# Four-image attention pipeline on one core: output products ordered by PSUM banks, with one bank finished by TensorE and ScalarE

## The reference

```python
x_proj = jnp.einsum('mc,bchw->bmhw', w_in, x)             # 128 channels -> 16
fs = fftshift(fft2(x_proj, norm='ortho'))
mag_avg = abs(fs).mean(axis=1)                            # energy by angle, 90 bins
# two strongest angles of an image choose a region; gain is 1.2, 1.0 or 0.8
fs_enh = fs * gain[:, None, :, :]
x_enh = ifft2(ifftshift(fs_enh), norm='ortho').real
out = jnp.einsum('cm,bmhw->bchw', w_out, x_enh)           # 16 -> 128 channels
return x + out
```

## Time and profile before

| | us |
|---|---|
| median of 3 runs | 278.42 (278.32 to 278.46) |
| the profiled execution | 278.63 |
| its span | 276.8 |
| TensorE busy | 264.9 |
| ScalarE busy | 184.7 |
| VectorE busy | 174.3 |
| the eight transfers to `out`, issue to landing, each | 2.1 |

### The profile page before, as it was taken

How to read it: one execution, slowest core, us unless ns; L and a number is a source line. 1 busy time by engine, 2 the same in 40 slices (tenths; PEclk the granted TensorE clock), 3 DMA queues, 4 the chain that set the end, 5 groups by cost and what they waited for, 6 DMA issues and landing times.

```text
span 276.8 us, 4058 instructions
## 1 busy us (share of the span) xinstructions
PE 264.9 (96%) x1328; PEld 157.1 (57%) x1331; DVE 174.3 (63%) x297; ACT 184.7 (67%) x355; POOL 63.3 (23%) x97
## 2 busy tenths in 40 slices
PE   7999999999999999999999999988999998899993
PEld 2864666457655665563667535844545546664573
DVE  4686769687645743276776978777325247646773
ACT  1584477887887667665787577988846758647430
POOL 2016018300400002537821300110003607500000
PEclk9999999999999999999999999999999999999999
DMA  5990000000000010000000000000000000000026
GB/s 170 281 305 3 0 0 4 23 26 26 4 0 0 0 54 2 0 1 1 3 0 1 0 2 1 4 1 0 0 1 0 2 0 4 1 1 2 1 78 227
DMA packets 4573, 8.52 MB, mean 31 GB/s; under 512 B 1250, under 2 KB 2018, under 8 KB 4554
## 3 DMA queue, kind: packets, MB, share of 16 engines
q1 hardware_dynamic: 4554, 8.27, 9.1%
HBM read 5.60 MB, written 2.10 MB: 28 GB/s over the span
## 4 chain that ended last, share of the span: by engine, by line
PE 87%; ACT 4%; DVE 3%; DMA 2%; issue 1%; SPq 0%; DVEq 0%; ACTq 0%
PE psum L366 84%; DMA qs<-row 2%; DMA xin<-in_x 1%; PE psum L491 1%; DVE nmax L890 1%; DVE xl L852 1%; SPq L354 0%; ACT L748 0%; ACT L742 0%; ACT e L661 0%; DVE x L871 0%; ACT qs L676 0%; DVEq L199 0%; PE psum L467 0%; ACT x2T L698 0%
## 5 line engine op out<-in xcount | busy, mean ns | idle before, releaser
L366 PE MATMUL psum<-e,v 128*128 128x512 f32 x128 | 60.0, 593 | 0.0
L890 DVE TENSOR_REDUCE nmax<-psum 128x1 f32<-128x1024 f32 x32 | 38.5, 1221 | 19.6 <-PE psum L366 19.6
L661 ACT ACTIVATE e<-psum,nmax 128x1024 f32<-128x1024 f32 x32 | 35.7, 1115 | 18.0 <-issue 12.7
L861 DVE TENSOR_REDUCE nmax<-psum 128x1 f32<-128x1024 f32 x32 | 39.0, 1221 | 11.5 <-PE psum L366 10.9
L694 ACT ACTIVATE e<-psum 128x1024 f32<-128x1024 f32 x32 | 32.2, 1024 | 14.1 <-PE psum L366 13.6
L684 ACT ACTIVATE psum<-psum,nmax 128x1024 f32<-128x1024 f32 x32 | 34.9, 1091 | 8.5 <-DVE nmax L890 8.5
L366 PEld LDWEIGHTS psum<-e,v 128*128 128x128 f32 x128 | 23.7, 189 | 18.9 <-issue 15.9
L1051 POOL CAST qs<-qs 32x512 fp32r<-32x512 f32 x16 | 9.7, 606 | 102.9 <-ACT qs L676 102.1
L366 PE MATMUL psum<-qs,ks 96*128 96x512 f32 (+1 forms) x96 | 30.1, 415 | 2.4 <-DMA qs<-row 2.0
L366 PE MATMUL psum<-ks,qs 96*128 96x512 f32 (+1 forms) x96 | 31.1, 428 | 1.0 <-ACT e L694 0.7
L366 PE MATMUL psum<-e,v0n 128*64 128x512 f32 x128 | 30.9, 605 | 0.0
(11 more groups left out here) (174 smaller groups left out, 409.8 us busy)
## 6 DMA issues: line engine op xcount, KB each, us to landing
out<-xin SPq DMA_DIRECT2D x8, 256.0 KB, 2.1
xin<-in_x SPq DMA_DIRECT2D x3, 512.0 KB, 6.2
twist<-in_twist_in SPq DMA_DIRECT2D x1, 768.0 KB, 8.6
zz<-in_region_in SPq DMA_DIRECT2D x2, 360.0 KB, 6.7
xin<-in_x SPq DMA_DIRECT2D x2, 256.0 KB, 2.7
untwist<-in_untwist_in SPq DMA_DIRECT2D x1, 512.0 KB, 8.2
e<-in_near_in SPq DMA_DIRECT2D x1, 272.0 KB, 8.8
rw<-in_rows_w SPq DMA_DIRECT2D x1, 256.0 KB, 2.7
```

The costliest lines, as they stand in the source:

```text
L366: return nc.tensor.matmul(o, lhsT, rhs, start=start, stop=stop, skip_group_check=skip)
L661: inc(go(e0[:, E0_AT[b, i], :], t[:, :], ACT.Exp, bias=nmax0[z][:, i:i + 1], accum_out=sum0[z][:, i:i + 1]), "e0_ready", b)
L861: inc(vec.tensor_reduce(nmax0[z][:, i:i + 1], t[:, :], AX.X, ALU.max, negate=True), "nmax0_ready", b)
L890: inc(vec.tensor_reduce(nmax1[z][:, i:i + 1], t[:, :], AX.X, ALU.max, negate=True), "nmax1_ready", b)
```

## The change

Six things change.

- `wout.b.i` does the four blocks j = 0 to 3 of half i, so that each part fills one bank.
- `y.b.i` waits for its own part of `wout` and adds one bank: columns 128 i to 128 i + 127 of each group of 256 of `xin`.
- Image 3's second bank is begun by a new step `xadd.3.1`, which multiplies `xin` of image 3 (the bank's columns) by the identity; `wout.3.1` adds its products to that. `xadd.3.0` only begins the banks.
- `y.3.1` leaves VectorE: ScalarE copies the bank to `xin`, and then issues one transfer of image 3 from its own queue.
- SyncE waits for both `y` of an image before it issues either half, and issues only the first half of image 3.
- Five warm steps (27 to 31) go, some banks of the tail are others, and on VectorE `hart.3.0` stands earlier.

```diff
@@ the last steps of PE_TEXT
-    "... s2.3.0@4 warm.0.27@7 warm.0.28@6 warm.0.29@3 selT.0.0@5 "
-    "warm.0.30@7 region.0.0@5 energy.1.0@6 coefT.0.0@7 coefT.1.0@5 i1.0.0@0 ... "
+    "... s2.3.0@4 xadd.3.0@6 selT.0.0@5 region.0.0@5 energy.1.0@3 "
+    "coefT.0.0@1 xadd.3.1 coefT.1.0@5 i1.0.0@0 ... "
@@ def banks():
-            first, j = SHARES[name]
+            first, j = ("xadd", 0) if (name, b) == ("wout", B - 1) else SHARES[name]
@@ SyncE
             for b in range(B):
-                for h in range(2):
+                wait(sp, "y_ready", b, 0 if b == B - 1 else 1)
+                if b == B - 1:
+                    sp.wait_ge(y_last, 1)
+                for h in range(1 if b == B - 1 else 2):
                     hc = slice(h * HALF, (h + 1) * HALF)
-                    wait(sp, "y_ready", b, h)
                     sp.dma_start(out[b][:, hc], xin[:, b, hc]).then_inc(out_written, 16)
@@ TensorE
+                elif name == "xadd":
+                    if i == 0:
+                        begin(step)
+                        continue
+                    wait(pe, "x3_ready", b, 1)
+                    t = tile(step)
+                    xv = xin[:, b, :].rearrange("p (a j w) -> p j a w", j=CH, w=W)
+                    mm(t[:, HALF:N], ident, xv[:, CH // 2:CH], True, False, True)
...
-                    for j in (2 * i, 2 * i + 1):
-                        for k in range(2):
-                            half, o = slice(k * BM, (k + 1) * BM), k * HALF + j * P
-                            last = mm(t[:, o:o + P], woutT[half, j, :], xe[z][half, :], True, True)
+                    half = slice(i * BM, (i + 1) * BM)
+                    for j in range(CH // 2):
+                        o = i * HALF + j * P
+                        last = mm(t[:, o:o + P], woutT[half, j, :], xe[z][half, :], b < B - 1 or i == 0, True, b == B - 1 and i == 1)
@@ ScalarE
+                if name == "y":
+                    wait(act, "y_full", b, 1)
+                    banked = slice(i * CH // 2, (i + 1) * CH // 2)
+                    tv = tile(("wout", b, 0)).rearrange("p (j a w) -> p a j w", j=CH, w=W)[:, :, banked]
+                    xv = xin[:, b, :].rearrange("p (a j w) -> p a j w", j=CH, w=W)[:, :, banked]
+                    go(xv, tv, ACT.Copy).then_inc(y_last, 1)
+                    act.wait_ge(y_last, 1)
+                    wait(act, "y_ready", b, 0)
+                    act.dma_start(out[b][:, HALF:N], xin[:, b, HALF:N]).then_inc(out_written, 16)
@@ VectorE
-                    wait(dve, "y_full", b, 1)
+                    wait(dve, "y_full", b, i)
                     wait(dve, "x3_ready", b, 1)
-                    tv = tile(("wout", b, 0)).rearrange("p (j a w) -> p a j w", j=CH, w=W)[:, 2 * i:2 * i + 2]
-                    xv = xin[:, b, hc].rearrange("p (a j w) -> p a j w", j=CH, w=W)
+                    banked = slice(i * CH // 2, (i + 1) * CH // 2)
+                    tv = tile(("wout", b, 0)).rearrange("p (j a w) -> p a j w", j=CH, w=W)[:, :, banked]
+                    xv = xin[:, b, :].rearrange("p (a j w) -> p a j w", j=CH, w=W)[:, :, banked]
                     inc(vec.tensor_tensor(xv, tv, xv, ALU.add), "y_ready", b)
```

More of the change, by code:

```diff
@@ L159 @@
 ONE_BANK = "warm gap xconv qkproj asproj chan chanT xproj xturn s1 s2 energy selT region coefT i1 i2 shift1 shift2".split()
-SHARES = dict(mix=("mix", 0), mid=("mix", 0), attH=("attH", 0), joinc=("joinc", 0), joina=("joinc", 0), joinb=("joinc", 0), wout=("wout", 0))
+SHARES = dict(mix=("mix", 0), mid=("mix", 0), attH=("attH", 0), joinc=("joinc", 0), joina=("joinc", 0), joinb=("joinc", 0), wout=("wout", 0), xadd=("xadd", 0))
 def banks():
@@ L301, in conv_seq @@
         x_in = [ctx.enter_context(nc.semaphore(f"x_in{b}")) for b in range(B)]
-        split_0, x_first, fill_ready = [
-            ctx.enter_context(nc.semaphore(n)) for n in ("split_0", "x_first", "fill_ready")]
+        split_0, x_first, fill_ready, y_last = [
+            ctx.enter_context(nc.semaphore(n)) for n in ("split_0", "x_first", "fill_ready", "y_last")]
         weights_in, const_in, near_sem, table_in, region_sem, out_written = [
@@ L638, in _ @@
                 hc = slice(i * HALF, (i + 1) * HALF)
-                if name == "sqrt":
+                if name == "y":
[7 more added lines that the diff above has]
+                    act.dma_start(out[b][:, HALF:N], xin[:, b, HALF:N]).then_inc(out_written, 16)
+                elif name == "sqrt":
                     act.wait_ge(s["small_dve"][0], 1)
```

## The result

The changed kernel takes 283.93 us (median of 4 runs, 283.58 to 288.26), the kernel before took 278.44 beside it (4 runs, 278.32 to 280.39). The ratio is 1.0176, 95% interval 1.0120 to 1.0232. It leaves out the run of 288.26, whose mean granted clock was 0.971 where the other three had 0.994; the experiments come back to it. The profiled execution lasted 283.91, its span is 282.1 (before: 276.8).

What follows compares the result with a forecast made beforehand. TensorE was taken to bound the kernel, busy 87% of the span. The terms 1.79 + 1.56 + 0.52 - 0.07 - 0.70 + 0.60 = 3.70 us on a median of 278.42 gave 282.1 us; the range was 280.9 to 282.9.

Steps and rivals of the forecast that it cites:

- (1): `wout` by banks: passes no longer share slots; four lone steps add 1.79 us, `wout.2` and `wout.3` add 1.56.
- (2): Identity product `xadd.3.1` between the two `coefT`: partly covered by TensorE's wait, delays `i1.0` by 0.52 us.
- (3): Five warm products removed: `region.0` starts sooner, a gain of 0.07 us; lost cover for the clock costs 0.
- (5): Image 3's end: first bank's addition runs beside the second bank's products, only ScalarE's copy follows; 0.70 us gained.
- (6): Image 3's transfers: issued together on full DMA engines, the second lands later; 0.60 us lost.
- rival E: Tail from 260 us: without the warm products the granted clock falls to 1.2 GHz, 285 us or more; 2%.
- Rival A: `wout`: the two passes of one product pair, so order by banks costs nothing; +0.35, 278.8 us; 6%.
- B: As Rival A, with `xadd` hidden and both queues landing together; only the shorter end remains, -0.8, 277.6 us; 6%.
- rival C: `wout.2` and `wout.3`: their halves still overlap, so 1.56 us goes, 280.6 us; 8%.
- D: `wout`: weight loads of consecutive passes in one half aren't hidden, 64 passes add 6.4 us, 288 us; 2%.
- the 76%: The chance given to the forecast itself, 281.4 to 282.9 us by its own bounds.

Runs made afterwards that it cites:

- a1: The changed kernel with its five warm products put back; median 285.39 us in four runs, 284.38 us and ratio 1.0147 in six more.
- b1: The kernel before without its last five warm products, nothing else changed; median 280.08 us, ratio 1.0041.
- a4: a3 with the identity product moved earlier, into the place of warm steps 27 to 29 ahead of `selT.0`; median 279.05 us, ratio 0.9998.
- b2: The kernel before with only `wout` by banks; median 282.19 us, ratio 1.0123 in four runs, 281.94 us and 1.0124 in six more.
- a3: a1 with `wout` alternating the two halves again, both additions of image 3 waiting for the second part; median 279.52 us, ratio 1.0003.
- d1: b2 with output products 128 rows high, zeros in the other half of `woutT`; median 281.60 us, ratio 1.0105.
- a2: a1 with the identity product moved earlier, into the place of warm steps 27 to 29; median 282.06 us, ratio 1.0086.
- after_again: The changed kernel, unaltered, run six more times; median 288.74 us.
- b3: The kernel before with only image 3's two transfers issued together from two queues after the last addition; median 279.65 us, ratio 1.0011.

## Why the prediction was wrong

It had the direction and most of the size, 282.1, and missed 283.93 by 1.8; the range ended at 282.9. By its steps, in the two profiled executions (the last instruction's end 276.8 and 282.1, 5.3 apart):

| step | forecast | measured | from |
|---|---|---|---|
| (1) lone `wout` steps, four | 1.79 | 1.78 | 0.71 to 1.16 each |
| (1) `wout.2`, `wout.3` | 1.56 | 1.10 | 1.16 to 1.71 each |
| (2) `xadd.3.1` | 0.52 | 0.53 | transpose to `i1.0`: 0.70, 1.23 in a1 |
| (3) release of `selT.0`, `region.0` | -0.07 | +0.20 | `sel` ready to `selT.0`: 0.06 to 0.26 |
| (3) clock | 0 | 1.58 | `s2.3` to `i2.0`: 6.41 in a1, 7.99 |
| (5) end | -0.70 | -0.70 | 1.34 to 0.64 |
| (6) transfers | 0.60 | 0.74 | end of the last addition or copy to the end of the span |
| upstream | 0 | 0.08 | start of `s2.3` |
| sum | 3.70 | 5.31 | |

Without the clock the measured terms give 3.73, the forecast's sum. That they meet so closely is in part luck: -0.46 in the neighbouring `wout` steps, +0.27 in the release and +0.14 in the transfers nearly cancel. The step that failed is **(3), "Cost 0" for the lost cover of the clock**, and with it rival E, given 2%, came in a smaller form. I had argued that the clock is 1.00 in the last 3.7 us without a matmul and that the holes would stay below 1 us. The first is true, the second nearly so (the hole ahead of `selT.0` is 1.15, with 0.34 behind it), but the end of a program shows the clock behind the last matmul, not what a thinned stretch does to the products behind it. What could have warned me was the busy time in the stretch: without its four warm products it went from 2.35 to 1.24 of 2.70, nearly half. It would not have settled it, for the kernel before has a stretch with 1.68 of 2.70 at 178.8 and no fall in that run. But the 2% had no row of that stretch behind it. And E's price was too coarse: "half speed over some 11 us" against one stretch of 3.4, worth 1.6. a1 and b1 show the cause from both sides; a4 shows that three of the warm products aren't needed if other work fills their place.

**Passes.** The slot of 0.112 held: 0.45 for a lone step, shown by b2 and undone by a3. Rival A (pairs are the two passes of one product) and B fell with it. Two numbers of the rivals don't add up as written: D's +6.4 comes on top of the 3.70, 288.5 and not 288, and the bounds named with the 76% reach down to 280.9 and not 281.4. Neither bears on the outcome. For neighbouring halves I had assumed one shared slot; the measured 1.71 has eight of 0.112 less three, so that rival C (halves overlap) is right for a part of it. That is a size and not a mechanism, 0.23 a pair. D (loads not hidden) fell: the pitch within one half is 0.112. "TensorE: Matmul & The Clock Gate" of the Trainium skill says in the table "Why this matters for your kernels" that a single product of small K lasts as long as one of full K, and that the gain is in tiles running together; d1 and b2 agree, 1.13 and 1.16 for eight passes.

**`xadd`** cost what was forecast, by a1 against the kernel before. **The selection of the first group** has a step that I missed: the changed order puts the waits of `xadd.3.0`'s banks on `selT.0`, as the rows of the order show (`filled7`, `filled6` beside `sel_ready_0`), and 0.2 more pass between `sel` and the transpose. a1 still has it (0.26 from `sel` to the transpose). b1, with a hole nearly as long (0.95) and the old waits, has 0.06, and in a4 and a2, where the waits of `xadd.3.0` fall on `xadd.3.1`, it is 0.09. That points to the waits; no run takes them alone. **The end** and **the transfers** are sized right, the second by 0.14 too low; ScalarE's issue takes 0.41 where SP's takes 0.33, and the two land 2.7 and 2.8 after their issue.

One thing no step held: 6 of 10 runs of the changed kernel ended 4 to 8 us later still, by the late fall. The forecast had no term for a fall behind a stretch in which TensorE is recorded busy.

## What to carry to other kernels

A product that feeds nothing may be holding the clock: before one is taken out, look at what TensorE would still do in the stretch it stands in, and give a rival with the stretch behind it at half speed a real chance; 3.4 us at 0.50 cost 1.4 to 1.6 here. Products over 64 rows in alternating halves of the array share a slot, in one half they don't, so an order by PSUM banks that sorts them apart needs twice the slots: eight passes went from 0.72 to 1.16. If a helper product must go in, put it where TensorE waits for another engine anyway.

## What the runs showed of the hardware

- The granted clock fell to 0.50 for 3.4 us after a stretch with TensorE busy 1.24 of 2.70 us (changed) or 2.10 of 3.50 us (b1), though no single hole was longer than 1.2 us. It stayed at 1.00 behind 1.68 of 2.70 us in the profiled run of the kernel before and fell behind 1.67 of 2.70 in d1's.
- It also fell with TensorE recorded busy 6.64 of 6.80 us ahead of it (after_again, the one profile of it). By the mean clock this comes in 13 of 43 runs of kernels whose 64-row products ran one at a time and in none of 80 runs of the other experiments; the kernel before had one such run of 82.
- By the mean clock, the fall near 184 us comes in about four of ten runs of the kernel before (32 of 82), costs 1.9 us and didn't answer to work added in the tail.
- Eight 128-column fp32 passes of 64 rows in one half last 1.16 us, of 128 rows 1.13 to 1.16, of 64 rows in alternating halves 0.72. Behind 128-row passes the next step starts a little sooner (1.06 against 1.09 after the first pass; d1, b2).
- Two 256 KB transfers issued together from two queues land 2.5 and 2.7 us after their issue (b3), and 2.7 and 2.8 where the issues are 0.07 us apart (changed kernel); one alone takes 2.1.
